# Attention stage of a two-layer kernel: the raw outputs' transposes, the output steps and the sums over values move to later places of the next batch's turn

## The chip, the cores and the metric

The kernel runs on one core of one Trainium2 chip. The metric is the device time of one execution in microseconds (us).

## What is computed

Two layers over 16 sequences of 256 tokens with 128 features. Layer 0 is a gated linear recurrence times a mixture of 64 experts. Layer 1, cut to what matters, is attention with 16 heads of 8 features, times a gate from a mixture of 16 experts:

```python
scores = jnp.einsum('bhqd,bhkd->bhqk', q, k) * scale
scores = jnp.where(causal[None, None], -jnp.inf, scores)
attn = jax.nn.softmax(scores, axis=-1)
out = jnp.einsum('bhqk,bhkd->bhqd', attn, v)
out = out.transpose(0, 2, 1, 3).reshape(b, s, E)
return out @ wo + bo
...
x = x + s * g
```

## The kernel before, in words

`layer0` runs the first layer, `layer1` the second. `layer1` has two parts. The first goes over 8 tiles of 512 tokens and makes queries, keys, the latent of the values and the gate. The second, the attention stage, goes over the 16 batches (sequences), and the change touches only this part.

A batch passes through three stages, and three batches are under way at once. In one turn (one call of `both` on each engine) stage a works on batch n+2, stage x on batch n+1 and stage o on batch n. A turn is cut into 18 places (`NU`, i = 0 to 17), and each engine goes through the places in order. The tables `X_AT`, `V_AT`, `QUERIES_AT`, `KEYS_AT` and the numbers `O_RAW` to `O_END` say at which place a step stands. The same tables are read by TensorE (PE), VectorE (DVE) and ScalarE (ACT), so a number moves a step on every engine that has a part in it. Engines work strictly in this order and meet through semaphores.

- Stage a, `a_unit`: at places 0 to 3 the units k0, q0, k1, q1: four matmuls each (L1406) copy keys or queries of 8 heads into PSUM, and ACT (k0, k1, L1341) or DVE (q0, q1, L1805) copies them out. A unit waits until the unit two before it has been read. At places 4 to 15 come the 12 max units (max 0 to max 11, two matmuls each into two alternating PSUM banks), each followed by a DVE reduction (L1813). Place 16 is the values' projection v, and place 17 the unit m: 8 transposes (L1532) of the row maxima, which ACT and DVE then copy into two rows of the queries (L1350, L1796). `masked_queries` (ACT, L1360) and `masked_keys` (DVE, L1827) stand at the places of their tables.
- Stage x: eight score units, x0 to x7, at the places `X_AT`. PE makes the transposed scores (two matmuls on `l_wqk` or `l_xt` with `l_big`) in one PSUM pair of banks, ACT takes the exponential (L1369), POOL cuts it causally (L1255). PE can make the next one only when ACT has read the last. Four sums over values, v0 to v3 (`values`, L1576, 16 small matmuls), stand at the places `V_AT`. They write PSUM banks 6 and 7, and v0 waits until the output of the batch before is done (`s_done`).
- Stage o: at `O_RAW` ACT copies banks 6 and 7 to SBUF (L1375, 128x1024). At `O_TB` PE transposes that back (L1587, 8 matmuls). At `O_NORM` DVE divides by the sums (L1835, L1839). At `O_OT` PE transposes the result (L1592), at `O_WO` ACT copies it (L1378) and PE multiplies by `wo` and adds the bias (four matmuls, L1406 with `l_wo` and `l_bo`). At `O_END` DVE makes the output (L1844, L1848), and SP stores it (L1207) and loads the inputs of the batch two later.

On PE the order within a place is: the score unit, the sum over values, the o step, the a unit. On ACT it is: the o step, the a unit, the masked queries, the exponential. On DVE: the o step, the a unit, the masked keys.

```python
O_RAW, O_TB, O_NORM, O_OT, O_WO, O_END = 0, 1, 2, 4, 6, 7
...
both(n * 2 + 2, n * 2, 0, 0, n)
both(n * 2 + 3, n * 2 + 1, 1, 1, n)
```

Fourteen turns have all of stages a, x and o. Before them are two with no stage o (the second has stages a and x), and behind them one with stages x and o, and one with stage o alone.

Of the kernel before, what the change touches and what calls it, by code (L numbers as in the profile page):

```python
# [907 lines left out]
def layer1(nc, d, scratch, out_dram, sem):  # L908

    y_dram, g_dram, x2_dram, g1_dram = scratch  # L910
    with ExitStack() as ctx:
# [184 lines left out]
        N_ACT, N_DVE = sum(BY_ACT), sum(BY_DVE)  # L1096
        MAX0, NM, XU = 4, 12, 8
        QUERIES_AT, KEYS_AT = {4: (0, 0), 7: (0, 2), 10: (1, 0), 13: (1, 2)}, {1: (0, 0, 4), 5: (1, 0, 2), 7: (1, 2, 2)}
        X_AT, V_AT = (3, 4, 6, 7, 9, 10, 12, 13), (9, 11, 14, 17)

        O_RAW, O_TB, O_NORM, O_OT, O_WO, O_END = 0, 1, 2, 4, 6, 7

        def max_rows(par, j):

# [763 lines left out]
def build(nc, d, out):  # L1868

    def scratch(name, *shape):  # L1870
        return nc.dram_tensor(name, shape, F32).ap()

    z = scratch("z_scratch", NT, NS, BS, H0, TP, ZC)
    y = scratch("y_scratch", NT, P, TP, HD0)
    g0 = scratch("g0_scratch", NT, NS, P, D)
    x2 = scratch("x2_scratch", B, N, D)
    g1 = scratch("g1_scratch", B, N, D)
    with ExitStack() as ctx:
        def sem(name):
            return ctx.enter_context(nc.semaphore(name))  # L1880

        layer0(nc, d, (z, y, g0), sem)
        layer1(nc, d, (y, g0, x2, g1), out, sem)
# [56 lines left out]
```

## Time and profile before

| | us |
|---|---|
| median of three runs | 2169.27 (2168.54 to 2169.32) |
| the profiled execution's own time | 2166.51 |
| its span, first to last instruction | 2164.8 |
| granted TensorE clock, mean over the span | 0.889 of full |
| busy: PE / DVE / ACT / POOL | 1634.9 / 1583.1 / 1134.5 / 1019.8 |

Busy times add up over stages with different limits. A row of the timeline reads: start in us, duration in us, engine, line, operation, tile written<-tiles read, shapes, count of merged instructions, and in brackets the idle time of the engine before it and what ended it. Duplicate buffers have one name. A matmul's duration includes its way through the array, so the distance from start to start is shorter.

### The profile page before, as it was taken

Reading aid. Unit: us, or ns where it says so; the run is one execution under the profiler, and the core shown is the slowest. Engines: PE = TensorE matmul, PEld = TensorE weight load, DVE = VectorE, ACT = ScalarE, POOL = GpSimd, SP = SyncE. Lnnn points to the kernel's source line nnn. Section 1 sums busy time; section 2 is a strip of 40 time slices with the busy share of each in tenths; the row PEclk is TensorE's granted clock in tenths of the full one; section 3 lists DMA queues with packets and bytes.
Section 4 is the critical chain, followed back from the end, with each engine's and each line's share of the span. In section 5 each row is a group of like instructions: output and inputs, shape, how many; then the busy total and the mean of one; then the engine's idle time right before and its main releaser. Section 6 shows DMA issues by size and latency. Waiting matters only on the chain. (4 is left out here: it accounts for less than half of the span.)

```text
span 2164.8 us, 32713 instructions
## 1 busy us (share of the span) xinstructions
PE 1634.9 (76%) x8418; PEld 1187.9 (55%) x8418; DVE 1583.1 (73%) x4335; ACT 1134.5 (52%) x1811; POOL 1019.8 (47%) x1114
## 2 busy tenths in 40 slices
PE   3186786886858758597684299898999988878876
PEld 2154454554535535364452298787888865555554
DVE  3199989999999999999998444444444457667763
ACT  1265464664636646366453154544545546666664
POOL 2766877677777867777795000000000003323332
PEclk8598888898988979789898599999999989999997
DMA  4410020110200102002000511001110000000000
GB/s 85 100 40 15 1 65 1 28 38 1 64 0 21 43 1 64 0 11 48 1 10 10 126 21 25 19 13 26 21 25 10 16 25 16 15 15 15 22 15 13
DMA packets 140675, 58.82 MB, mean 27 GB/s; under 512 B 94711, under 2 KB 135148, under 8 KB 140524
## 3 DMA queue, kind: packets, MB, share of 16 engines
q1 hardware_dynamic: 140524, 57.19, 11.8%
q8 instruction: 48, 0.79, 0.2%
q14 instruction: 103, 0.84, 0.1%
HBM read 36.05 MB, written 21.10 MB: 26 GB/s over the span
## 5 line engine op out<-in xcount | busy, mean ns | idle before, releaser
L594 PE MATMUL pb<-hid,wd 128*128 128x512 f32 x528 | 301.4, 656 | 192.0 <-POOL hid L406 191.1
L402 POOL TENSOR_TENSOR hid<-act_g,act_u 128x512 f32<-128x512 f32 x256 | 328.2, 1282 | 163.5 <-ACT act_c L518 148.3
L518 ACT ACTIVATE act_g<-pb 128x512 f32<-128x512 f32 (+1 forms) x264 | 158.1, 599 | 371.2 <-PE pb L545 329.6
L406 POOL TENSOR_TENSOR hid<-hid,act_c 128x512 f32<-128x512 f32 x256 | 328.7, 1284 | 21.5 <-POOL hid L402 1.8
L1762 DVE SCALAR_TENSOR_TENSOR l_acc<-l_pb,l_gtok,l_acc 128x128 f32<-128x128 f32 x512 | 144.4, 344 | 257.0 <-PE l_pb L1406 256.7
L1321 ACT ACTIVATE l_hid<-l_pb,l_cols 128x512 f32<-128x512 f32 x256 | 169.4, 688 | 183.1 <-PE l_pb L1406 182.7
L543 PE MATMUL pb<-xt_hi,wg_hi 128*128 128x512 f32 (+1 forms) x264 | 190.3, 721 | 91.3 <-ACT act_g L518 91.3
L1406 PEld LDWEIGHTS l_pb<-l_big,l_hid 128*128 128x128 f32 x2048 | 247.1, 192 | 10.6
L1406 PE MATMUL l_pb<-l_big,l_hid 128*128 128x128 f32 x2048 | 247.9, 275 | 0.0
L1406 PE MATMUL l_pb<-l_xt,l_big 128*128 128x512 f32 x768 | 219.1, 420 | 26.5 <-DVE l_rope L1694 24.9
L594 PEld LDWEIGHTS pb<-hid,wd 128*128 128x128 f32 x528 | 101.7, 206 | 246.5 <-POOL hid L406 220.1
L1235 POOL TENSOR_TENSOR l_ql<-l_rope,l_qh 128x512 f32 x8 | 10.3, 1284 | 434.0 <-ACT l_qh L1315 434.0
L861 DVE TENSOR_TENSOR products<-zr,rs 128x512 f32<-128x512 f32 x256 | 174.5, 682 | 20.2 <-POOL zr L355 10.4
L864 DVE TENSOR_REDUCE rs<-products 128x32 f32<-128x512 f32 x256 | 175.4, 685 | 0.0
L862 DVE TENSOR_TENSOR products<-zr,rs 128x512 f32<-128x512 f32 x256 | 173.8, 679 | 0.0
L1406 PEld LDWEIGHTS l_pb<-l_xt,l_big 128*128 128x128 f32 x768 | 138.3, 194 | 56.9 <-DVE l_rope L1694 23.5
L518 ACT ACTIVATE act_u<-pb 128x512 f32<-128x512 f32 (+1 forms) x264 | 157.8, 598 | 21.6 <-PE pb L545 13.2
L1813 DVE TENSOR_REDUCE l_mrow<-l_pb 128x2 f32<-128x512 f32 (+1 forms) x192 | 127.9, 686 | 50.9 <-PE l_pb L1406 50.4
L1247 POOL TENSOR_TENSOR l_turnstile<-l_turnstile 128x1 f32<-128x1 f32 x128 | 27.9, 218 | 272.0 <-ACT l_big L1369 209.5
L518 ACT ACTIVATE act_c<-pb 128x512 f32<-128x512 f32 x256 | 152.6, 596 | 0.0
L543 PEld LDWEIGHTS pb<-xt_hi,wg_hi 128*128 128x128 f32 (+1 forms) x264 | 54.0, 204 | 164.0 <-ACT act_g L518 68.3
L652 PE MATMUL pb<-cwt,sel 128*128 128x512 f32 x256 | 107.3, 419 | 22.4 <-ACT cwt L468 22.4
(314 smaller groups left out, 3881.6 us busy)
## 6 DMA issues: line engine op xcount, KB each, us to landing
z_scratch<-zs SPq DMA_DIRECT2D x128, 81.0 KB, 3.0
zr<-z_scratch SPq DMA_DIRECT2D x8, 1296.0 KB, 8.1
x_sb<-in_L_attn_x_dram SPq DMA_DIRECT2D x32, 64.0 KB, 2.1
g_scratch<-zs SPq DMA_DIRECT2D x8, 256.0 KB, 2.8
y_scratch<-yo SPq DMA_DIRECT2D x8, 256.0 KB, 2.1
l_xs<-in_L_attn_x_dram SPq DMA_DIRECT2D x32, 64.0 KB, 1.9
l_ys<-y_scratch SPq DMA_DIRECT2D x128, 16.0 KB, 1.8
l_gs<-g_scratch SPq DMA_DIRECT2D x8, 256.0 KB, 3.0
```

The costliest lines, as they stand in the source:

```text
L402: pool.tensor_tensor(hid1[:, :], g, u, ALU.mult).then_inc(s_h1, 1)
L406: pool.tensor_tensor(hid[:, (p + par) % 2, :], hid1[:, :], c, ALU.mult).then_inc(s_h, 1)
L518: act.activation(dst, pb[0:n, what, :], ACT.Silu if what == 0 else ACT.Copy).then_inc(s_ev, 1)
L543: pe.matmul(out, l_hi, r_hi, start=first, stop=False, skip_group_check=True)
L594: last = pe.matmul(pb[:, SUM, :], wd[0:n, p, :], hid[0:n, (p + par) % 2, :], start=(p == 0), stop=(p == PAIRS), skip_group_check=True)
L861: dve.tensor_tensor(products[:, 2:4], two(ZG), twice, ALU.mult).then_inc(s_st, 1)
L862: dve.tensor_tensor(products[:, 0:2], two(ZF), twice, ALU.mult).then_inc(s_st, 1)
L864: dve.tensor_reduce(rs[:, 3, 0:2], products[:, 2:4], AX.X, ALU.add).then_inc(s_st, 1)
L1321: act.activation(hid[:, r % HR, :], pb[:, 2 + r % 3, :], ACT.Relu, bias=cols[:, r:r + 1]).then_inc(s_hid, 1)
L1406: return pe.matmul(out, l, r, start=start, stop=stop, skip_group_check=True)
L1762: dve.scalar_tensor_tensor(out=acc[:, s, :], in0=pb[:, 5 + e % 2, sub], scalar=gtok[par][:, s, e:e + 1], in1=acc[:, s, :], op0=ALU.mult, o ...
L1813: dve.tensor_reduce(dst, pb[:, 2 + m % 2, :].rearrange("p (j n) -> p j n", j=heads), AX.X, ALU.max).then_inc(s_ua_dve, 1)
```

## The change

Only two lines of the tables change. The transposes of the raw output go from place 1 to 3, the division from 2 to 4, the transposes of the result from 4 to 6, the output product (and ACT's copy before it) from 6 to 8, and the end from 7 to 9. The sums over values v0, v1 and v2 go from places 9, 11 and 14 to 11, 13 and 15; v3 stays at 17. No instruction is added or removed.

```diff
-        X_AT, V_AT = (3, 4, 6, 7, 9, 10, 12, 13), (9, 11, 14, 17)
+        X_AT, V_AT = (3, 4, 6, 7, 9, 10, 12, 13), (11, 13, 15, 17)
 
-        O_RAW, O_TB, O_NORM, O_OT, O_WO, O_END = 0, 1, 2, 4, 6, 7
+        O_RAW, O_TB, O_NORM, O_OT, O_WO, O_END = 0, 3, 4, 6, 8, 9
```

First place, PE at places 0 to 3 of a turn in the loop, before. `l_kh` marks units k0 and k1, `l_qh` q0 and q1, `l_rope` the raw output, `l_big,l_wqk` a score unit; what a row waits for stands behind it.

```order
L1406 MATMUL l_pb<-l_kl,l_rep 128x256
L1583 REGISTER_ALU
L1587 MATMUL l_pb<-l_ident,l_rope 128x128 [waits a_raw_out_copied]
L1587 MATMUL l_pb<-l_ident,l_rope 128x128 x7
...
L1406 MATMUL l_pb<-l_qh,l_rep 128x256
...
L1406 MATMUL l_pb<-l_kh,l_rep 128x256 [waits a_unit_read_by_act]
...
L1406 MATMUL l_pb<-l_big,l_wqk 128x512 [waits a_probs_exp]
L1406 MATMUL l_pb<-l_big,l_wqk 128x256
```

The same place now:

```order
L1406 MATMUL l_pb<-l_qh,l_rep 128x256
...
L1406 MATMUL l_pb<-l_kh,l_rep 128x256 [waits a_unit_read_by_act]
...
L1406 MATMUL l_pb<-l_big,l_wqk 128x512 [waits a_probs_exp]
L1406 MATMUL l_pb<-l_big,l_wqk 128x256
L1587 MATMUL l_pb<-l_ident,l_rope 128x128 [waits a_raw_out_copied]
L1587 MATMUL l_pb<-l_ident,l_rope 128x128 x7
```

Units q0 and k1 and the score unit x0 now stand ahead of the eight transposes.

Second place, ACT at places 6 to 9, before. `l_big<-l_pb 128x768` is an exponential, `l_big<-l_xt,l_qmask` the masked queries, L1378 the copy of the transposed result.

```order
L1369 ACTIVATE l_big<-l_pb 128x768 [waits a_scoresT_in_psum]
L1378 ACTIVATE l_big<-l_pb 128x256 [waits a_outT_in_psum]
L1365 REGISTER_ALU
L1369 ACTIVATE l_big<-l_pb 128x768 [waits a_scoresT_in_psum]
...
L1365 REGISTER_ALU
L1369 ACTIVATE l_big<-l_pb 128x768 [waits a_scoresT_in_psum]
L1365 REGISTER_ALU
L1369 ACTIVATE l_pt<-l_pb 128x768 [waits a_scoresT_in_psum]
```

The same place now:

```order
L1369 ACTIVATE l_big<-l_pb 128x768 [waits a_scoresT_in_psum]
...
L1365 REGISTER_ALU
L1369 ACTIVATE l_big<-l_pb 128x768 [waits a_scoresT_in_psum]
L1378 ACTIVATE l_big<-l_pb 128x256 [waits a_outT_in_psum]
L1365 REGISTER_ALU
L1369 ACTIVATE l_pt<-l_pb 128x768 [waits a_scoresT_in_psum]
```

The copy went from behind the second exponential to behind the fourth.

Third place, PE at places 13 to 17, before. `l_kb` marks a max unit, `l_hid` a sum over values.

```order
L1406 MATMUL l_pb<-l_big,l_xt 128x512 [waits a_probs_exp]
L1406 MATMUL l_pb<-l_big,l_xt 128x256
L1406 MATMUL l_pb<-l_kb,l_xt 128x512 [waits a_unit_read_by_dve]
L1406 MATMUL l_pb<-l_mask_b,l_ident_b 128x512
L1576 MATMUL l_pb<-l_pt,l_hid 32x256 [waits a_probs_causal]
...
L1406 MATMUL l_pb<-l_wv,l_big 128x128 [waits a_latent_copied,a_unit_read_by_act]
L1406 MATMUL l_pb<-l_wv,l_big 128x128
L1576 MATMUL l_pb<-l_pt,l_hid 32x256 [waits a_probs_causal]
L1576 MATMUL l_pb<-l_pt,l_hid 32x256 x3
L1576 MATMUL l_pb<-l_pt,l_hid 32x128 x4
L1532 MATMUL l_pb<-l_ident,l_mhl 128x128 [waits a_max_split]
```

The same place now:

```order
L1406 MATMUL l_pb<-l_big,l_xt 128x512 [waits a_probs_exp]
L1406 MATMUL l_pb<-l_big,l_xt 128x256
L1576 MATMUL l_pb<-l_big,l_hid 32x256 [waits a_probs_causal]
...
L1406 MATMUL l_pb<-l_kb,l_xt 128x512 [waits a_unit_read_by_dve]
L1406 MATMUL l_pb<-l_mask_b,l_ident_b 128x512
...
L1576 MATMUL l_pb<-l_pt,l_hid 32x256 [waits a_probs_causal]
...
L1576 MATMUL l_pb<-l_pt,l_hid 32x256 [waits a_probs_causal]
...
L1532 MATMUL l_pb<-l_ident,l_mhl 128x128 [waits a_max_split]
```

Three sums over values instead of two now lie between the last score unit x7 and the transposes of unit m.

## Rows read from the trace of the kernel before

**Rows 1.** Timeline of ACT, raw copies: first and last full turn, a long turn
```profile
1801.13 1.02 ACT L1375 ACTIVATE l_rope<-l_pb 128x1024 f32<-128x1024 f32 x1
...
1991.37 1.02 ACT L1375 ACTIVATE l_rope<-l_pb 128x1024 f32<-128x1024 f32 x1
2016.34 1.02 ACT L1375 ACTIVATE l_rope<-l_pb 128x1024 f32<-128x1024 f32 x1
...
2135.60 1.02 ACT L1375 ACTIVATE l_rope<-l_pb 128x1024 f32<-128x1024 f32 x1
```

**Rows 2.** Waits of PE over the 14 full turns: us in total, times, longest
```profile
PE l_pb L1587 <- ACT l_rope L1375: 39.0, 14, 2.8
```

**Rows 3.** Timeline of PE, one turn, places 0 to 6
```profile
2013.91 0.36 PE L1406 MATMUL l_pb<-l_kh,l_rep 128*128 x1
...
2017.41 1.10 PE L1587 MATMUL l_pb<-l_ident,l_rope 128*128 128x128 f32 x8 [2.79 <-ACT l_rope L1375]
2018.27 0.36 PE L1406 MATMUL l_pb<-l_qh,l_rep 128*128 x1
...
2018.82 0.28 PE L1406 MATMUL l_pb<-l_kh,l_rep 128*128 x1
...
2019.30 0.51 PE L1406 MATMUL l_pb<-l_big,l_xt 128*128 128x512 f32 x2
...
2020.94 0.61 PE L1406 MATMUL l_pb<-l_big,l_xt 128*128 128x512 f32 x2 [0.45 <-ACT l_big L1369]
```

**Rows 4.** Timeline of ACT, the same turn, places 0 to 7
```profile
2017.56 0.67 ACT L1341 ACTIVATE l_wqk<-l_pb,l_kspare 128x512 fp32r<-128x512 f32 x1
2019.49 0.69 ACT L1341 ACTIVATE l_wqk<-l_pb,l_kspare 128x512 fp32r<-128x512 f32 x1 [1.26 <-PE l_pb L1406]
2020.08 0.81 ACT L1369 ACTIVATE l_big<-l_pb 128x768 f32<-128x768 f32 x1
...
2022.00 0.81 ACT L1369 ACTIVATE l_big<-l_pb 128x768 f32<-128x768 f32 x1
2022.69 0.39 ACT L1378 ACTIVATE l_big<-l_pb 128x256 f32<-128x256 f32 x1
2023.78 0.81 ACT L1369 ACTIVATE l_big<-l_pb 128x768 f32<-128x768 f32 x1 [0.70 <-PE l_pb L1406]
...
2025.71 0.80 ACT L1369 ACTIVATE l_big<-l_pb 128x768 f32<-128x768 f32 x1
```

**Rows 5.** Timeline of PE, the same turn, places 6 to 17 (excerpts)
```profile
2023.15 0.59 PE L1406 MATMUL l_pb<-l_big,l_xt 128*128 128x512 f32 x2
2023.58 0.38 PE L1406 MATMUL l_pb<-l_wo,l_big 128*128 128x128 f32 x2
...
2024.39 0.47 PE L1406 MATMUL l_pb<-l_kb,l_xt 128*128 128x512 f32 x1
...
2026.57 0.61 PE L1406 MATMUL l_pb<-l_big,l_xt 128*128 128x512 f32 x2
2027.11 0.86 PE L1576 MATMUL l_pb<-l_big,l_hid 128*32 128x256 f32 x16
2027.90 0.49 PE L1406 MATMUL l_pb<-l_kb,l_xt 128*128 128x512 f32 x1
...
2028.28 0.59 PE L1406 MATMUL l_pb<-l_big,l_xt 128*128 128x512 f32 x2
...
2030.85 0.59 PE L1406 MATMUL l_pb<-l_big,l_xt 128*128 128x512 f32 x2
...
2032.34 0.62 PE L1406 MATMUL l_pb<-l_big,l_xt 128*128 128x512 f32 x2 [0.55 <-ACT l_pt L1369]
...
2036.64 1.09 PE L1532 MATMUL l_pb<-l_ident,l_mhl 128*128 128x128 f32 x8 [0.27 <-DVE l_mhl L1818]
```

**Rows 6.** Table of stretches: the start of a long turn; the clock is third from the end
```profile
1991.60:1997.60 6.00, 5.15 (x22) 4.78 (x22) 2.38 (x7) 3.11 (x6) 0.00 (x0) 0.51 0.00 0
```

**Rows 7.** Timeline of ACT, first exponential of the turn without stage a
```profile
2139.32 0.81 ACT L1369 ACTIVATE l_big<-l_pb 128x768 f32<-128x768 f32 x1 [2.70 <-PE l_pb L1406]
```

## The prediction

> **What bounds the kernel now.** I read the page first, then the table of waits over the attention stage, then the timelines of PE, ACT and DVE over one turn. The change touches only the 16 turns of this stage. The raw copies of ACT come once a turn: from 1801.13 to 2135.60 us lie 14 full turns, 334.5 us [rows 1]. One turn, beginning with unit k0 at 2013.91, which I call time 0, reaches the transposes of unit m at 22.73 [rows 3, 5]. These are eight transposes, which take 0.86 from start to next start as the eight of L1587 do (2017.41 to 2018.27, [rows 3]), so a turn is 23.59. Fourteen would be 330.3. The 4.2 left are three long turns like that from 1991.37 to 2016.34, which took 24.97 [rows 1], 1.38 more. At the start of that turn the granted clock was 0.51 [rows 6], the lower level of 1.2 GHz, after TensorE had waited.
>
> The largest wait of TensorE is the one for the raw copy: 39.0 us in 14 turns, 2.79 each [rows 2, 3]. It is what the change goes at. But it is not all loss that can be taken back. The ACT queue ahead of it (unit m's copies, then the raw copy) is untouched, and unit k0's own copy stands behind the raw copy on ACT, at 3.65 [rows 4]. A second chain runs through the turn: score unit on PE, exponential on ACT, next score unit. The reader is to see in [rows 5] that PE is busy from x4 to x7 with that chain nearly in step, and that from x7 to m (18.43 to 22.73) it has only 0.27 of waiting.
>
> **The start of the turn.** q0 now follows k0 at once, but k1 must wait until ACT has read k0. ACT's copy starts at 3.65 as before and takes 0.67; PE starts about 0.05 after the end of what it waits for (exponential 2020.08 + 0.81, PE 2020.94, [rows 3, 4]). So k1 starts at 4.37 instead of 4.91: of the 2.79 wait, only 0.54 is gained, and PE waits as long, for k0's copy. From k1, by distances in [rows 3, 4]: k1's copy +0.67, first exponential +0.59, at 5.63 instead of 6.17. The transposes of L1587 cost 0.86 behind x0, and q1 follows. x1 then starts at about 4.85 + 0.46 + 0.86 + 0.55 = 6.7 instead of 7.03, in time for the second exponential: 5.63 + 1.92 = 7.55 (masked queries between them). Third score unit x2: +0.86 = 8.41 instead of 9.24. The wait of the result's transposes for DVE (places 2 to 4) goes too, since DVE now has all of two places.
>
> **The middle.** Third exponential: +0.63 (2023.15 to 2023.78) = 9.04. Fourth: +1.93 = 10.97, against 11.80 before, so 0.83 is won so far. Now the loss. ACT's copy L1378 stood behind the second exponential and was ready when PE came to the output product. It now stands behind the fourth, at 10.97 + 0.69 = 11.66, and takes 0.39 [rows 4]. PE stops for it ahead of max 4. The product starts at 12.10 and takes 0.81 (2023.58 to 2024.39, [rows 5]), so max 4 starts at 12.91. Before, the product stood behind x2 and max 4 had gone well ahead of x4 (12.66). What is queued behind this wait: max 4, hence DVE's reductions, and x4. x4: +0.38 = 13.29 instead of 12.66. With v0 gone from place 9, x5 follows at the pace of the exponentials, 0.63 + 0.86 = 1.49 later, 14.78 instead of 14.37. From x5 to x6 stands the same work as before with v0 in v1's place; that took 2.57, of which up to 0.3 was waiting for DVE. I take 2.4: x6 at 17.2 instead of 16.94, x7 1.49 later at 18.7 instead of 18.43 [rows 5].
>
> **The end.** From x7 to m took 4.30 [rows 5]. v1 is added to it at 0.79 (2027.11 to 2027.90). The wait of 0.27 at m hides a part at most: 4.82 to 5.09; I take 4.9. So m starts at 23.6 instead of 22.73, and a turn costs **0.87 us more**. Ends for this term: 0.5, if the chain to x4 is faster by 0.1 and all small waits absorb; 1.3, if x4 to x6 keep their full delay of 0.4 to 0.6.
>
> **Other turns.** The turn with stages a and x alone gets v1 behind x7 but no product: +0.5. The turn with x and o alone: its first exponential (2139.32, [rows 7]) waited for the transposes and x0; now x0 goes ahead and it can start right behind the raw copy, at about 2136.7. Against this win of 2.6 stand the transposes ahead of x1 and the product behind the fourth exponential, so I take -0.7, ends 0 and -2. The last turn keeps its chain. Moves I cost at nothing: v0's wait for the finished output (end at place 9, v0 at 11, so two places of cover as before; without it DVE's lateness would land on PE), the store and the two loads on SP that follow the end some 2 to 3 us later (they are needed two turns on, over 40 us), and POOL, whose cuts keep their order.
>
> Sum: 14 x 0.87 = 12.2, + 0.5, - 0.7, makes **12.0 us**. On the profiled execution's 2166.5 that is 2178.5. The median of the runs stands 2.8 above that execution, so I forecast **2181.3**.
>
> **The clock.** Three of 14 turns were long, each after the wait of 2.79, which with unit k0 before it was the longest of the turn. The wait ahead of k1 will be from the end of q0 (about 1.2) to 4.37, 3.2 us, though q0 adds work before it. I keep three long turns in the sum; none is the lower bound (-4.1), all 14 the upper (+15). The Trainium skill ("TensorE: Matmul & The Clock Gate", Why this matters for your kernels) warns of long idle gaps between bursts of matmuls, since TensorE's clock then falls to the lower level. By that rule the longer wait should bring more long turns, up to the sum of rival 3; by the rows alone their number stays. The trace agrees as far as three turns go, and shows eleven waits of the same length without a fall.
>
> **The rivals.**
> 1. *The lead is kept, and the kernel is faster.* Up to the fourth exponential the change wins 0.83 a turn. If the last third followed the exponentials and not PE's own work, the next turn would start that much earlier: 14 x 0.83 = 11.6 less, 2157 to 2158. For it: PE waits for ACT ahead of x7 (0.55). It decides at the product: the lead survives only if PE gets there with the copy L1378 done, that is with x4 at 11.9 or so, and if v1 behind x7 is covered. Against it: ACT runs in order, so the copy can't pass the fourth exponential, and between x7 and m there are 0.27 to cover 0.79. Chance 0.08.
> 2. *Win and loss cancel.* The stop at the product shrinks to some tenths and v1 falls half into waits: 0 to 0.3 a turn, 2168 to 2173. Without the stop, x4 would come at 12.2, x7 no earlier than 17.4, m at 22.3, still within 0.5 of before. Chance 0.12.
> 3. *The clock falls in nearly every turn.* Then ten or so more turns pay 1.4: 2181.3 + 14 = 2195. For it the longer wait, against it q0's added work right before it, and that eleven of 14 waits of 2.8 changed nothing. The rule of the Trainium skill named above speaks for this rival. Chance 0.12.
>
> That the change does not what it says I exclude by the order of the instructions, which shows the moves on all engines.
>
> **How the numbers follow.** My forecast has 0.68; its own range is 14 x 0.5 to 14 x 1.3, two clock falls more or fewer: 2174 to 2190. A measurement of this kernel can tell about 0.2%, 4.3 us, so "the same" is 2165 to 2173.6. Faster 0.08; the same 0.12; slower 0.68 + 0.12 = 0.80. The range leaves out rival 1, the lower part of 2 and the upper half of 3: 2170 to 2193.
>
> **What would show it.** In the profile after: PE's wait at L1587 gone, and one of about 3.2 us ahead of unit k1 for ACT L1341 in its place; first exponential 0.5 earlier in the turn; PE's wait for ACT L1378 of about 1 us in each of 14 turns, which before was none; 4.9 from x7 to m; raw copies 24.4 to 24.5 apart. The forecast is wrong if L1378 costs PE under 0.3, if x7 lies before 18.0, or if v1 fits between x7 and m without moving m. More than six turns over 25.5 would mean rival 3.

## The result and the profile after

The changed kernel takes 2192.19 us, the median of five runs (2184.49 to 2195.65), against 2168.54 us for the kernel before (2167.13 to 2169.32), timed side by side. The ratio is 1.0102, 95% interval 1.008 to 1.0124: slower by 1%, 23.7 us. The forecast was 2181.3 in a range of 2170 to 2193. The sign held. The time lies in the range, but only 0.8 us below its upper end, and the forecast loss of 12 us was half of the measured one.

The profiled execution has a span of 2190.5 us, 25.7 more than before. The waits of PE over the 14 full turns, against [rows 2] (us in total, times, longest):

```profile
PE l_pb L1406 <- ACT l_wqk L1341: 22.3, 7, 3.2
PE l_pb L1406 <- ACT l_xt L1341: 22.2, 7, 3.2
PE l_pb L1406 <- ACT l_big L1378: 15.6, 14, 1.1
PE l_pb L1406 <- ACT l_pt L1369: 15.3, 28, 0.6
PE l_pb L1406 <- ACT l_big L1369: 4.7, 14, 0.5
```

The wait at L1587 is gone from the list, and in its place stand 14 waits of 3.2 us for ACT's copy of unit k0 (L1341, two buffers, 44.5 us together against 39.0 before). The wait for ACT's copy L1378, 1.1 us in each turn, is new. Two waits for DVE are gone: that of the result's transposes (L1592, 7.5 us in all before) and that at unit m (L1532, 3.7 us).

The same turn's timeline of PE, at full clock, answers to [rows 3] and [rows 5]. Its time 0, unit k0, is 1877.86 (2.43 ahead of the raw copy at 1880.29, as in the turn of before in the rows). The rows are k1, x0, the raw output's transposes, the output product, the max unit behind it, x4, x7, v1 and unit m:

```profile
1882.24 0.39 PE L1406 MATMUL l_pb<-l_kh,l_rep 128*128 x1 [3.19 <-ACT l_wqk L1341]
...
1882.82 0.51 PE L1406 MATMUL l_pb<-l_big,l_xt 128*128 128x512 f32 x2
1883.17 1.04 PE L1587 MATMUL l_pb<-l_ident,l_rope 128*128 128x128 f32 x8
...
1890.09 0.49 PE L1406 MATMUL l_pb<-l_wo,l_big 128*128 128x128 f32 x2 [1.10 <-ACT l_big L1378]
...
1891.01 0.48 PE L1406 MATMUL l_pb<-l_kb,l_xt 128*128 128x512 f32 x1
...
1891.37 0.59 PE L1406 MATMUL l_pb<-l_big,l_xt 128*128 128x512 f32 x2
...
1896.53 0.61 PE L1406 MATMUL l_pb<-l_big,l_xt 128*128 128x512 f32 x2 [0.55 <-ACT l_pt L1369]
1897.08 0.86 PE L1576 MATMUL l_pb<-l_big,l_hid 128*32 128x256 f32 x16
...
1901.55 1.09 PE L1532 MATMUL l_pb<-l_ident,l_mhl 128*128 128x128 f32 x8
```

The timeline of ACT in the same turn, against [rows 4], with the first, second and fourth exponential and the copy L1378:

```profile
1883.61 0.80 ACT L1369 ACTIVATE l_big<-l_pb 128x768 f32<-128x768 f32 x1
...
1885.53 0.81 ACT L1369 ACTIVATE l_big<-l_pb 128x768 f32<-128x768 f32 x1
...
1888.97 0.80 ACT L1369 ACTIVATE l_big<-l_pb 128x768 f32<-128x768 f32 x1
1889.66 0.38 ACT L1378 ACTIVATE l_big<-l_pb 128x256 f32<-128x256 f32 x1
```

Read from time 0, the steps of the forecast stand against it like this:

| step, us from unit k0 | before | forecast | after |
|---|---|---|---|
| k1 | 4.91 | 4.37 | 4.38 |
| first exponential | 6.17 | 5.63 | 5.75 |
| fourth exponential | 11.80 | 10.97 | 11.11 |
| output product | 9.67 | 12.10 | 12.23 |
| x4 | 12.66 | 13.29 | 13.51 |
| x7 | 18.43 | 18.7 | 18.67 |
| unit m | 22.73 | 23.6 | 23.69 |
| whole turn | 23.59 | 24.46 | 24.54 |

The raw copies of ACT, against [rows 1], show the rest: the first, two a full-speed turn apart, the two of a long turn, and the last:

```profile
1802.47 1.02 ACT L1375 ACTIVATE l_rope<-l_pb 128x1024 f32<-128x1024 f32 x1
...
1880.29 1.02 ACT L1375 ACTIVATE l_rope<-l_pb 128x1024 f32<-128x1024 f32 x1
1904.83 1.02 ACT L1375 ACTIVATE l_rope<-l_pb 128x1024 f32<-128x1024 f32 x1
...
1930.43 1.02 ACT L1375 ACTIVATE l_rope<-l_pb 128x1024 f32<-128x1024 f32 x1
1956.98 1.02 ACT L1375 ACTIVATE l_rope<-l_pb 128x1024 f32<-128x1024 f32 x1
...
2161.78 1.02 ACT L1375 ACTIVATE l_rope<-l_pb 128x1024 f32<-128x1024 f32 x1
```

Only three of the 14 turns last 24.54, with a mean granted clock of 1.00. The other eleven last 25.6 to 25.7 (mean clock 0.93) or 26.5 to 26.6 (0.87). In them the clock falls late in the wait ahead of k1 or just behind it. The table of stretches shows one of them behind the wait: the granted clock, third from the end, is 0.50, the lower level of 1.2 GHz. Matmuls then take half as long again or nearly double, the transposes 1.91 instead of 1.04 us:

```profile
1932.40:1938.40 6.00, 6.00 (x23) 5.13 (x23) 3.12 (x9) 3.48 (x5) 0.93 (x4) 0.50 0.00 0
```

```profile
1932.38 0.58 PE L1406 MATMUL l_pb<-l_kh,l_rep 128*128 x1 [3.19 <-ACT l_wqk L1341]
...
1934.04 1.91 PE L1587 MATMUL l_pb<-l_ident,l_rope 128*128 128x128 f32 x8
```

So the 25.7 us divide as follows. The 14 turns at full clock: 14 x (24.54 - 23.59) = 13.3. Long turns: the 14 turns last 359.3 us (1802.47 to 2161.78), 15.7 more than 14 x 24.54; before it was 4.2; difference 11.5. Ahead of the first raw copy 1.3, behind the last -0.5. The 1.3 is no more than two executions of the same instructions differ by: up to the first raw copy e7 and e8 below run the same code and took 1798.06 and 1801.40.

### The profile page after: what moved, and what is told of

Its sections match the earlier page's. It is cut to its first block and busy times, and to the rows that moved or that the text cites. A ratio compares the mean times of both kernels' runs of the same rounds, so it can differ in the third digit from the quotient of the medians.

```text
span 2190.5 us, 32706 instructions
## 1 busy us (share of the span) xinstructions
PE 1648.5 (75%) x8418; PEld 1203.0 (55%) x8418; DVE 1586.2 (72%) x4335; ACT 1135.1 (52%) x1811; POOL 1025.2 (47%) x1114
## 5 line engine op out<-in xcount | busy, mean ns | idle before, releaser
L1406 PEld LDWEIGHTS l_pb<-l_big,l_hid 128*128 128x128 f32 x2048 | 247.1, 192 | 10.5
L1406 PEld LDWEIGHTS l_pb<-l_xt,l_big 128*128 128x128 f32 x768 | 137.8, 193 | 56.0 <-DVE l_rope L1694 23.6
```

The lines of the kernel that those rows point to most:

```text
L1406: return pe.matmul(out, l, r, start=start, stop=stop, skip_group_check=True)
```

## The experiments

Two theories were tested. In the expectations "theory A" is the schedule's part, as far as the run bears on it, and "clock theory" the other. **The schedule:** a turn loses at two places, at the stop of PE for the copy L1378 and at v1, which comes behind x7. **The clock:** the quiet stretch at the start of a turn lets the clock fall, and this, not the late places, makes turns long. All times are medians, timed beside the kernel before. "Full-speed turn" is the distance of two raw copies with the clock up in between, 23.59 before and 24.54 in the changed kernel; a long turn is one in which it fell. Each trace is of one execution, and so is each count of long turns. The diffs of e1 to e4 and of e7 are against the kernel before.

### e1: the sums over values alone

```diff
-        X_AT, V_AT = (3, 4, 6, 7, 9, 10, 12, 13), (9, 11, 14, 17)
+        X_AT, V_AT = (3, 4, 6, 7, 9, 10, 12, 13), (11, 13, 15, 17)
```

> Only the sums over values move (places 11, 13, 15, 17); the steps of stage o stay where they were. Theory A (a sum over values that comes behind x7 costs nearly its whole 0.79 us, less the 0.2 to 0.3 that PE waited at m): x7 to m 4.8 to 4.9 instead of 4.30, a full-speed turn 24.1 to 24.2 instead of 23.6, PE's wait at L1587 stays 2.8, three long turns as before; time 8 us over before, about 2176.5. Rival (all of the loss comes from the stop at the output product, the sums over values hide): turn 23.6, time as before, 2168.5 +- 2.

Measured: 2182.86 us, ratio 1.0068 (1.0051 to 1.0085). Timeline of PE, x7 to m, and of ACT, two raw copies around that full-speed turn:

```profile
1843.67 0.62 PE L1406 MATMUL l_pb<-l_big,l_xt 128*128 128x512 f32 x2 [0.55 <-ACT l_pt L1369]
1844.22 0.86 PE L1576 MATMUL l_pb<-l_big,l_hid 128*32 128x256 f32 x16
...
1848.70 1.09 PE L1532 MATMUL l_pb<-l_ident,l_mhl 128*128 128x128 f32 x8
```

```profile
1827.66 1.02 ACT L1375 ACTIVATE l_rope<-l_pb 128x1024 f32<-128x1024 f32 x1
...
1851.98 1.02 ACT L1375 ACTIVATE l_rope<-l_pb 128x1024 f32<-128x1024 f32 x1
```

With unit k0 at 1825.23, x7 stands at 18.44 as before, x7 to m takes 5.03 instead of 4.30, and the turn 24.32. So v1 behind x7 costs 0.73 a turn by itself, a little over the 0.5 to 0.6 expected. The rival falls. The time is 15.7 us over before where 8 was expected. In the trace, 16.1 us over, the schedule makes 10.2 (14 x 0.73), the long turns 2.9 more than before (7.1 against 4.2) and the parts ahead of and behind the 14 turns 3.0. Nine turns, not three, were long, although PE's wait at L1587 was 2.8 as before. The clock theory in its simple form (a longer wait, more long turns) does not cover that.

### e2: the steps of stage o late, v1 again ahead of x7

v0 stays at place 11, since it must come behind the output's end at 9; v1 stands at 12, right ahead of x7, and v2 at 14 as before.

```diff
-        X_AT, V_AT = (3, 4, 6, 7, 9, 10, 12, 13), (9, 11, 14, 17)
+        X_AT, V_AT = (3, 4, 6, 7, 9, 10, 12, 13), (11, 12, 14, 17)
...
-        O_RAW, O_TB, O_NORM, O_OT, O_WO, O_END = 0, 1, 2, 4, 6, 7
+        O_RAW, O_TB, O_NORM, O_OT, O_WO, O_END = 0, 3, 4, 6, 8, 9
```

> The steps of stage o at the new places, the sums over values at 11, 12, 14, 17: v1 again ahead of x7, v0 as late as its wait for the output needs. Theory A (two separate costs, the stop at the product and v1 behind x7): the stop of 1.1 us stays, x7 to m back at 4.3, a full-speed turn 24.1, 0.4 to 0.5 under the changed kernel. Rival 1 (the stop alone is the loss): turn 24.5 as in the changed kernel. Clock theory (the 3.2 us wait ahead of k1, not the late places, makes turns long): most turns still long, 5 or more of 14; time 2180 to 2188. Against it: long turns back to three, 2176.

Measured: 2180.28 us, ratio 1.0062 (1.0044 to 1.0079). The stop stays (PE for L1378: 15.6 us, 14 times), and from x7 to m it is 4.26 us again. The full-speed turn is 24.00, read from the only one, the first:

```profile
1800.73 1.02 ACT L1375 ACTIVATE l_rope<-l_pb 128x1024 f32<-128x1024 f32 x1
1824.73 1.02 ACT L1375 ACTIVATE l_rope<-l_pb 128x1024 f32<-128x1024 f32 x1
```

Getting v1 back ahead of x7 gives 0.54 of the 0.95. Alone, the two parts cost 0.73 and 0.41; together 0.95, less than their sum. Thirteen turns were long. That count is one execution's: the ten executions of e2 took 2169.32 to 2190.05 us, the shortest with a mean granted clock of 0.889 and the profiled one, 2186.76, with 0.876. So how often the clock falls differs between executions of one kernel.

### e3: the early steps moved, the product left at place 6

```diff
-        O_RAW, O_TB, O_NORM, O_OT, O_WO, O_END = 0, 1, 2, 4, 6, 7
+        O_RAW, O_TB, O_NORM, O_OT, O_WO, O_END = 0, 3, 4, 5, 6, 7
```

> The raw output's transposes at place 3 and the division at 4 as in the change, the result's transposes at 5, but the output product and its ACT copy stay at 6, the end at 7, the sums over values at 9, 11, 14, 17. Theory A: no stop at the product (copy L1378 stands ahead of the third exponential again), the lead of 0.5 to 0.8 up to the fourth exponential is kept in part, a full-speed turn 23.1 to 23.3 instead of 23.6, so -5 us by schedule. PE's wait ahead of k1 3.2 as in the changed kernel. Clock theory (this wait makes more turns long): 6 to 11 long turns and the win is given back, 2165 to 2176. Rival (long turns come from something in the late places): three long turns, 2163.

Measured: 2172.39 us, ratio 1.0018 (1.0009 to 1.0028). The full-speed turn is 23.26 (again the first and only one), so the transposes at place 3 are a win of 0.33 when the product keeps its place. But 13 of 14 turns were long. The 14 turns took 345.5 us, 19.9 more than 14 x 23.26, which ate the schedule's gain of 4.6. Both theories hold here; the rival, which wanted three long turns, falls. The profiled execution, 2175.46, is the slowest of ten, so 13 is at the high end.

### e4: also ACT's raw copy behind unit k0's copy

```diff
-        O_RAW, O_TB, O_NORM, O_OT, O_WO, O_END = 0, 1, 2, 4, 6, 7
+        O_RAW, O_TB, O_NORM, O_OT, O_WO, O_END = 1, 3, 4, 5, 6, 7
```

> As e3, and ACT's raw copy at place 1, that is behind unit k0's copy instead of ahead of it. Theory A (the start of a turn is bound by ACT: unit m's copies, raw copy, k0's copy, k1): k1 0.9 us earlier, PE's wait ahead of it 2.2 to 2.3 instead of 3.2, a full-speed turn 22.2 to 22.5; with few long turns the time is 2145 to 2151. Rival (the transposes at place 3 then wait for the raw copy and x0 and x1 do not come earlier): turn 23.1 as in e3.

Measured: 2160.18 us, ratio 0.9975 (0.9961 to 0.9989). Waits of PE, and two raw copies of a full-speed turn:

```profile
PE l_pb L1406 <- ACT l_wqk L1341: 16.9, 7, 2.4
```

```profile
1800.96 1.02 ACT L1375 ACTIVATE l_rope<-l_pb 128x1024 f32<-128x1024 f32 x1
1823.49 1.02 ACT L1375 ACTIVATE l_rope<-l_pb 128x1024 f32<-128x1024 f32 x1
```

The wait ahead of k1 is 2.4 instead of 3.2 and the turn 22.53, 0.73 under e3: the start of a turn is bound by the ACT queue, and the rival (23.1 as in e3) falls. The time missed its expectation by 9 us or more; it had assumed few long turns, and twelve were long in spite of the shorter wait.

### e5 and e6: the wait filled with matmuls that nobody reads

e5 is the changed kernel, e6 the kernel before; the fillers write PSUM bank 4, which the next score unit overwrites. They stand only in the 14 full turns. The diff is that of e5; in e6 nine of them stand at place 1.

```diff
+                    if i == 2 and ba is not None and bx is not None and bo_ is not None:
+                        pe.wait_ge(s_pt, bx * XU)
+                        for _ in range(10):
+                            mm(pb[:, 4, :], rep[:, 0, 0, :], rep[:, 1, :, :].rearrange("p g r -> p (g r)"))
                     if bo_ is not None:
                         o_unit(bo_, i)
```

> The changed kernel with ten matmuls of 128x512 whose result nobody reads between q0 and k1 in each full turn: about 2.2 us of the 3.2 that PE waits ahead of k1, so nothing later moves at full clock. Clock theory (long turns come from the quiet stretch at a turn's start): long turns vanish, all turns near 24.5, 11 to 15 us under the changed kernel, time 2177 to 2181; the schedule's part, 13 us, stays. Rival (the clock falls for another reason, or the fillers cost as much as they save): long turns stay, 2190 to 2195.

> The kernel before with nine such matmuls behind k0, in its wait of 2.8 us ahead of L1587. Clock theory: its three long turns vanish, 4 us less, 2163. Rival: three or more long turns stay, 2167 or more.

Measured: e5 2177.67 us, ratio 1.0046 (1.0031 to 1.0061); e6 2161.22 us, ratio 0.9978 (0.9969 to 0.9988). Tables of stretches over the full turns, e5 and then e6 (clock third from the end):

```profile
1802.80:2146.50 343.70, 286.37 (x2228) 196.26 (x2226) 235.93 (x435) 225.15 (x337) 110.54 (x336) 1.00 0.06 16
```

```profile
1799.90:2130.30 330.40, 288.43 (x2215) 190.35 (x2213) 233.97 (x435) 225.16 (x336) 107.14 (x336) 1.00 0.06 17
```

The clock stays up throughout, and all 14 turns last 24.53 to 24.57 in e5, 23.55 to 23.67 in e6. So the clock theory holds and both rivals fall. The added work made the kernel before 5.7 us faster. The changed kernel went from 23.7 to 10.8 us over the kernel before timed beside it, 12.9 us; the plain difference of its medians, which were timed apart, is 14.5. This settles the split of the 14 turns: with no long turn on either side they take 343.7 and 330.5 us from first to last raw copy, so the change still costs 13.2 by its schedule. The rest of the loss within these turns, 11.6 of 24.8, is the clock. For the whole kernel the split is less sharp: with fillers the two medians are 16.5 us apart and the two traces 19.5, so that 3 to 6 us lie outside the 14 turns, where there are no fillers. In the traces 3.0 of them are ahead of the first raw copy, within what executions differ by there, and 2.3 in the turn with x and o (21.03 in e5, 18.73 in e6).

### e7 and e8: places chosen by what was learned

```diff
-        X_AT, V_AT = (3, 4, 6, 7, 9, 10, 12, 13), (9, 11, 14, 17)
+        X_AT, V_AT = (3, 4, 6, 7, 9, 10, 12, 13), (9, 12, 15, 17)
...
-        O_RAW, O_TB, O_NORM, O_OT, O_WO, O_END = 0, 1, 2, 4, 6, 7
+        O_RAW, O_TB, O_NORM, O_OT, O_WO, O_END = 1, 3, 3, 4, 6, 7
```

The division and the raw output's transposes both stand at place 3. e8 adds seven fillers at place 2.

> Places chosen by the mechanism: ACT's raw copy at 1 (behind k0's copy), transposes and division at 3, result's transposes at 4, product at 6, end at 7, sums over values at 9, 12, 15, 17 (v1 in the stop ahead of x7). Theory A: a full-speed turn 21.3 to 22.0, under e4's 22.5; with the clock falling in most turns as in e4 about 2145 to 2152. Rival (nothing is won over e4 because DVE's division at 3 holds up q1's copy): turn 22.5 or more.

> As e7, with seven matmuls whose result nobody reads between q0 and k1. Clock theory: long turns vanish, the time falls by another 10 to 15 us under e7, to 2133 to 2140. Rival: no gain over e7.

Measured: e7 2134.48 us, ratio 0.9857 (0.9841 to 0.9873); e8 2128.02 us, ratio 0.9822 (0.9806 to 0.9838). Two raw copies of a full-speed turn of e7, 21.43 apart, and PE from x6 to x7 in a later turn:

```profile
1843.37 1.02 ACT L1375 ACTIVATE l_rope<-l_pb 128x1024 f32<-128x1024 f32 x1
1864.80 1.02 ACT L1375 ACTIVATE l_rope<-l_pb 128x1024 f32<-128x1024 f32 x1
```

```profile
1963.94 0.61 PE L1406 MATMUL l_pb<-l_big,l_xt 128*128 128x512 f32 x2
1964.48 0.86 PE L1576 MATMUL l_pb<-l_big,l_hid 128*32 128x256 f32 x16
1965.27 0.49 PE L1406 MATMUL l_pb<-l_kb,l_xt 128*128 128x512 f32 x1
1965.65 0.59 PE L1406 MATMUL l_pb<-l_big,l_xt 128*128 128x512 f32 x2
```

v1 now stands between x6 and x7, where PE had waited 0.55 for the exponential, and the next score unit goes out without a wait. The full-speed turn is in its expected range of 21.3 to 22.0. Against e4, 22.53, four things were changed at once (the places of the division, of the result's transposes, of v1 and of v2), and no run separates them. Seven turns of e7 were long, where most had been assumed from e4, which is part of why e7 came in 10 us under its expected time. Its 14 turns took 307.0 us, those of e8, all at full clock, 299.3. The fillers took 6.5 us off the median, less than the 10 to 15 expected, since fewer turns had been long, and e8 too is 5 us under its expected time. Both versions beat both kernels.

### e9: the copy L1378 taken out of the way

e5 with ACT's copy one place earlier; PE's product stays at 8 and all sums over values stay late. The diff, against the changed kernel, is in ACT's `o_unit`; the fillers of e5 come on top.

```diff
-                if i == O_WO:
+                if i == O_WO - 1:
```

> The filled changed kernel (e5) with ACT's copy L1378 one place earlier, at 7, so that it stands ahead of the masked queries and the fourth exponential; PE's product stays at place 8. Theory A (the stop of 1.1 us is due to the copy's place on ACT): the stop falls under 0.3; x4, x7 and m come 0.8 to 1.2 earlier although all sums over values stay late: turn 23.3 to 23.7 instead of 24.54, 12 to 17 us under e5, 2161 to 2166. Rival (PE's work behind the product is the bound, the stop only stands where PE would wait anyway): turn 24.2 or more, under 5 us.

Measured: 2155.06 us, ratio 0.9935 (0.9914 to 0.9956). ACT, then PE with the product, x7 and m of the same turn (its time 0 is 1868.58):

```profile
1878.46 0.38 ACT L1378 ACTIVATE l_big<-l_pb 128x256 f32<-128x256 f32 x1
1878.72 1.33 ACT L1360 ACTIVATE l_big<-l_xt,l_qmask 128x512 fp32r<-128x512 f32 x2
1879.95 0.81 ACT L1369 ACTIVATE l_big<-l_pb 128x768 f32<-128x768 f32 x1
```

```profile
1879.52 0.38 PE L1406 MATMUL l_pb<-l_wo,l_big 128*128 128x128 f32 x2
...
1886.01 0.62 PE L1406 MATMUL l_pb<-l_big,l_xt 128*128 128x512 f32 x2 [0.55 <-ACT l_pt L1369]
...
1891.04 1.09 PE L1532 MATMUL l_pb<-l_ident,l_mhl 128*128 128x128 f32 x8
```

The stop is gone, x7 comes at 17.43 instead of 18.67, m at 22.46, and turns last 23.29 to 23.33, at the low end of what was expected; the time is 6 us under its expected range. One ACT instruction of 0.38 us, one place earlier, is worth 1.23 us a turn, 17.4 us over the 14 turns. The span fell by 22.0 (2177.0 to 2155.0); of the other 4.6, 1.8 lie ahead of the first raw copy, within what executions differ by there, and 2.8 behind the last. At full clock the change is then a gain of 0.3 a turn over the kernel before instead of a loss. The copy's move without the fillers was not run.

## Why the prediction was right, and where it was off

- **The start.** Right. The wait at L1587 only moved ahead of k1, where it ends with k0's copy on ACT; k1 came 0.53 earlier, 0.54 forecast. e4 shows the cause by moving it: with the raw copy behind k0's copy the wait shrank by 0.8.
- **The middle.** The lead up to the fourth exponential was 0.69 (11.11 against 11.80), 0.83 forecast. The stop at the product was right in place, size (1.1) and cause; e9 removed it, and 1.23 a turn with it. That x7 came at 18.67 where 18.7 was forecast is partly luck: x4 was 0.22 late and x5, at 15.01, 0.23 late, and from x5 to x6 it took 2.17 instead of 2.4.
- **v1 behind x7.** Right: x7 to m 5.02, forecast 4.9. e1 shows it alone.
- **A turn.** 0.95 more, 0.87 forecast. The small misses are the first exponential (0.12 later than forecast) and the product, which took 0.92 behind a wait, not 0.81.
- **The clock term.** This was the step that was mis-sized: "I keep three long turns in the sum". There were eleven, 11.5 us more, about half of the whole loss. By the prediction's own sign (more than six turns over 25.5) rival 3 had come true, at a chance of 0.12, and its 2195 is nearer to the measured 2192.19 than the forecast's 2181.3. What came was the forecast's schedule together with most of rival 3, which I should not have treated as alternatives. That the time still lies in the range, by 0.8 us, is luck: the range took in the lower half of rival 3, and one of the five executions, 2195.65, lies outside it. I also took the three long turns of before as a rate. They were not: e1 kept the wait of 2.8 and had nine, e4 shortened it to 2.4 and had twelve. In the changed kernel the lengths repeat every four turns (25.6, 26.5, 25.7, 24.54), so the falls are regular and not random from turn to turn. The fillers show that the quiet stretch is the cause; why it lets the clock fall in some turns and not in others, and how often, stays open. The rule of the Trainium skill ("TensorE: Matmul & The Clock Gate", Why this matters for your kernels), to avoid long idle gaps between bursts of matmuls, agrees with the traces, in which the clock stayed at 1.00 over the 14 turns of e5, e6 and e8 once the gap was filled. They show the fall for waits from 2.4 to 3.2 us.
- **The turn with stages x and o.** Off: the first exponential came right behind the raw copy as forecast (2162.92, 0.1 behind its end), but the distance from its raw copy to that of the last turn grew from 18.72 to 20.12, where I had -0.7. The clock was low through most of it (mean granted clock 0.58, against 0.74 before), and x4 waited behind the stop and the product (2171.51). This was made up in the last turn, where the last steps ran mostly at full clock (8.6 against 10.5 us; the transposes L1587 took 1.10 us against 1.86). So the sum of the two, -0.5 where -0.7 was forecast, is luck: it holds a loss and a gain by the clock, and the schedule's share was not measured.
- **Rivals 1 and 2.** Rival 1 (the lead is kept) did not come true. I had asked two things for it, no stop at the product and v1 covered; e9 has only the first and is already faster than before. Rival 2 had its numbers right (x4 at 12.2, x7 at 17.4, m at 22.3; e9: 12.23, 17.43, 22.46) and drew too little from them.

## What to carry to other kernels

When a step is moved to hide its wait, look up what stands at its new place on every engine that shares its number: PE's wait was cheap to move, and ACT's small copy, put behind a long exponential, cost more than was gained. A wait for an engine's queue moves with the next operand of that queue; to shorten it, reorder the queue that is late (the raw copy behind k0's copy, 0.7 us a turn), and put independent work where the engine waits in any case (v1 between x6 and x7). If turns of one loop have different lengths, compare full-clock turns first and count the rest apart. Count them in more than one execution if you can. A few matmuls into a free bank in the wait are a cheap test, and may be the fix.

## What the runs showed of the hardware

Waits of TensorE of 2.4, 2.8 and 3.2 us once in a turn each let the clock fall to its lower level in some turns, counted in one execution each: 3 of 14 (before) and 9 (e1) at 2.8, 11 (after), 13 (e2) and 13 (e3) at 3.2, 12 (e4) and 7 (e7) at 2.4. So the length of the wait alone does not give the number. With 7 to 10 matmuls of 128x512 in the wait it fell in none of 14 (e5, e6, e8, e9). A long turn cost 0.3 to 2.1 us over a full-speed one. A kernel got faster by matmuls whose result is thrown away, by 5.7 us before and about 13 us after the change.
